# Layer 0 of a graph network: TensorE fetches part of the rows that GpSimd gathers

## The reference

```python
h = x @ W
e = leaky_relu((h @ att_src)[src] + (h @ att_dst)[dst], 0.2)   # edges and self loops
e = exp(e - segment_max(e, dst)[dst])
alpha = e / segment_sum(e, dst)[dst]
x = layernorm(x + tanh(segment_sum(h[src] * alpha[:, None], dst) + bias))
h1 = gelu(x @ W_pre + b_pre)
y = x + segment_sum(h1[src] * edge_attr, dst)
x = layernorm(x + y + gelu(gelu(y @ W1 + b1) @ W2 + b2))
```

## Time and profile before

| | us |
|---|---|
| median of 3 runs (3724.31 to 3727.02) | 3726.49 |
| the profiled execution | 3724.54 |
| its span, first to last instruction | 3722.8 |
| GpSimd busy in the span | 2781.1 (75%) |
| VectorE busy | 2438.3 (65%) |
| TensorE busy | 2393.6 (64%) |
| ScalarE busy | 1283.2 (34%) |

### The profile page before, as it was taken

One profiled execution on the slowest core, in us unless ns is written; L12 is line 12 of the kernel. 1 busy time (PEld: TensorE's weight loads), 2 busy tenths in 40 slices (PEclk: granted clock), 3 DMA queues, 4 the chain that ended last, 5 costly groups with the idle time before them and its releaser, 6 DMA issues.

```text
span 3722.8 us, 66966 instructions
## 1 busy us (share of the span) xinstructions
PE 2393.6 (64%) x16704; PEld 1951.7 (52%) x16705; DVE 2438.3 (65%) x6240; ACT 1283.2 (34%) x3893; POOL 2781.1 (75%) x2950
## 2 busy tenths in 40 slices
PE   6433343434344444444445988989888989999888
PEld 3333333333333333333334777777776777777776
DVE  7444444444466666566666777777777788888886
ACT  5433343434445555555553111111111221111222
POOL 7777777777777777777775777777777777777776
PEclk7555555555555555555557999999999999999998
DMA  5222221222222222222223343443334343444332
GB/s 102 43 42 42 41 44 42 44 42 43 42 43 44 43 44 43 43 44 45 44 45 99 93 94 90 95 94 94 95 91 96 93 96 91 97 95 99 93 95 70
DMA packets 351632, 254.26 MB, mean 68 GB/s; under 512 B 254125, under 2 KB 279218, under 8 KB 351387
## 3 DMA queue, kind: packets, MB, share of 16 engines
q0 software_dynamic: 94016, 146.16, 17.8%
q1 hardware_dynamic: 242753, 99.71, 11.7%
q10 hardware_dynamic: 14618, 6.14, 0.6%
HBM read 244.43 MB, written 7.25 MB: 68 GB/s over the span
## 4 chain that ended last, share of the span: by engine, by line
POOL 60%; issue 24%; ACT 4%; DVE 4%; PE 3%; DMA 2%; ACTq 1%; DVEq 1%; POOLq 0%; SPq 0%
POOL rows L690 60%; ACT onehot L747 1%; DMA rows<-table,src_i 1%; DMA src_i<-in_src_dram 1%; PE bank L1086 1%; ACT L790 1%; ACTq L740 0%; ACT pair L767 0%; DVE score L1361 0%; PE bank L1029 0%; PE bank L962 0%; ACT rowu L796 0%; DVE bst L1399 0%; ACT unused L790 0%; DVE newp L1352 0%
## 5 line engine op out<-in xcount | busy, mean ns | idle before, releaser
L690 POOL DMA_INDIRECT rows<-table,src_i x2850 | 2694.8, 946 | 896.0 <-issue 859.5
L1086 PE MATMUL bank<-node,hot 128*128 128x288 bf16 x9310 | 1228.4, 294 | 28.1 <-issue 16.5
L995 PE MATMUL bank<-onehot,rows 128*97 128x72 f32 (+1 forms) x3048 | 584.9, 369 | 814.9 <-ACT onehot L777 814.9
L1086 PEld LDWEIGHTS bank<-node,hot 128*128 128x128 bf16 x9310 | 932.2, 101 | 282.4 <-issue 20.9
L995 PEld LDWEIGHTS bank<-onehot,rows 128*97 128x97 f32 x3048 | 530.8, 281 | 854.4 <-issue 792.5
L1505 DVE TENSOR_SCALAR hot<-node,key 128x642 bf16<-128x642 int16 x1862 | 870.3, 539 | 130.8 <-PE bank L1086 80.0
L900 ACT ACTIVATE pair<-dst_i 128x8 f32<-128x8 int32 x196 | 35.2, 180 | 1175.3 <-DVE rows L1531 904.3
L747 ACT ACTIVATE onehot<-iota,far_dst 128x72 f32 (+1 forms) x1564 | 384.4, 328 | 23.0
L1339 DVE SCALAR_TENSOR_TENSOR other<-onehot,bank 128x576 f32<-128x576 f32 (+1 forms) x196 | 121.9, 622 | 404.1 <-ACT bank L760 335.4
L1073 PE MATMUL bank<-onehot,rows 128*96 128x40 f32 (+1 forms) x3128 | 306.8, 256 | 88.4 <-DVE rows L1536 50.6
L1073 PEld LDWEIGHTS bank<-onehot,rows 128*96 128x96 f32 x3128 | 295.8, 170 | 110.1 <-issue 88.7
(11 more groups left out here) (204 smaller groups left out, 1931.1 us busy)
## 6 DMA issues: line engine op xcount, KB each, us to landing
attr<-in_edge_attr_dram SPq DMA_DIRECT2D x190, 336.0 KB
rows<-table,src_i POOLq DMA_INDIRECT x2850
node<-in_src_dram SPq DMA_DIRECT2D x195, 64.0 KB
attr<-in_edge_attr_dram SPq DMA_DIRECT2D x190, 48.0 KB
dst_i<-in_dst_dram SPq DMA_DIRECT2D x200, 4.0 KB
src_i<-in_src_dram SPq DMA_DIRECT2D x195, 4.0 KB
src_i<-in_src_dram SPq DMA_DIRECT2D x190, 3.5 KB
dst_i<-in_dst_dram SPq DMA_DIRECT2D x190, 3.5 KB
```

What stands on the lines that cost most here:

```text
L690: pool.indirect_dma_start(rows[:, u, j * width:(j + 1) * width], None, table, bass.IndirectOffsetOnAxis(ap=src_i[:, u, j:j + 1], axis=0))\
L995: last = pe.matmul(total[:, 0:w], rows0(u, it)[:, j, 0:D1], wide(weights, w)[:, j, :], start=j == 0, stop=j == most - 1)
L1086: last = pe.matmul(p_got[t], hot[:, c % HOTS, i, t * P:(t + 1) * P], tab[:, a, :, :].rearrange("p k d -> p (k d)"), start=a == 0, stop=a = ...
```

## The change

Layer 0 gets what layer 1 has. From round 4 on, TensorE fetches the last tile of the first two groups in a narrow round and of the first group in a wide one (`BOOKED0 = 2`, `booked_in`), and GpSimd gathers seven tiles of those groups (`booked0`).

- In rounds 1 and 2 `table0` is split into three bf16 parts in nine steps, one a group (`split0` on ScalarE, `split_rest0` on VectorE); the parts lie in `attr`, behind `x1` and in `hot`.
- Each round's fetch is made one round ahead, in ten pieces of 4 or 5 blocks (`PIECE0`), two a group. VectorE compares for one piece between L1344 and L1318 of the next group, and for the other at that group's end (`marks0`); TensorE multiplies both behind the group's last half sum (`fetch0`; 3 x 98 columns). At the end of a round VectorE waits for the last piece and adds the three parts into tile 7 of the slot (`taken0`); ScalarE's `given` of a booked group waits for that.
- SyncE loads the 128 (256) source indices of the fetched tiles, the same row to all partitions (`load_src0`), and ScalarE shortens them to 16 bits (`shorten_src0`). The indices of a booked group come in three loads instead of two (`load_split`).
- Two PSUM banks are made free: `p_topb` and `p_newp` move into bank 0, `p_node2` into bank 6, and TensorE's chunk work waits for ScalarE's Gelu of the chunk before.
- Rounds 0 to 3 are written out instead of 0 and 1, and the last two instead of the last; chunks are held until round 4 (`HELD`).

```diff
+BOOKED0 = 2
+FROM0 = 4
+ERA0 = 10
...
-        p_top, p_topb, p_newp = bank[0][0:WIN, 0:P], bank[1][:, 0:WIN], bank[1][:, P:P + WIN]
+        p_top, p_topb, p_newp = bank[0][0:WIN, 0:P], bank[0][:, P:P + WIN], bank[0][:, P + WIN:P + 2 * WIN]
...
-        p_node, p_node2 = bank[6], bank[7]
+        p_node, p_node2 = bank[6], bank[6]
+        p_got0 = [bank[i][:, 0:3 * D2] for i in (1, 7)]
...
+        def booked_in(e, w):
+            return BOOKED0 if narrow(e, w) else 1
+        def booked0(it, u, w):
+            return in_era(it) and u < booked_in(it, w)
+        def fetched_at(it, u, w):
+            return booked_in(era_at(it, u), w)
+        def era_at(it, u):
+            return it + 2 if u == SLOTS - 1 else it + 1
+        def pieces_at(u):
+            return (0, 1) if u == SLOTS - 1 else (2 * u + 2, 2 * u + 3)
...
-                    for j in range(TILES - (e is e1 and booked(it, u))):
+                    for j in range(TILES - (booked(it, u) if e is e1 else booked0(it, u, ws[0]))):
...
+                if booked0(it, u, w):
+                    act.wait_ge(q_out, it - FROM0 + 1)
                 act.activation(p_src, rows0(u, it)[:, :, D1], ACT.Copy).then_inc(t0.given, 1)
...
+            def split0(k):
+                if k > 0:
+                    act.wait_ge(h_rest, k)
+                    act.activation(table0_part(k - 1)[:, :, 1, :], table0_left(k - 1), ACT.Copy).then_inc(h_mid, 1)
+                if k < len(TABLE0):
+                    if TABLE0[k][2] is flat[2]:
+                        act.wait_ge(e0.free, 2 * SLOTS + SLOTS)
+                    act.activation(table0_part(k)[:, :, 0, :], table0_rows(k), ACT.Copy).then_inc(h_hi, 1)
+            def shorten_src0(it):
+                act.wait_ge(q_src, 16 * BOOKED0 * (it + 3 - FROM0))
+                if not first_era(it, SLOTS - 1):
+                    act.wait_ge(q_hot, (it + 2 - FROM0) * ERA0)
+                act.activation(src16_0, src_all0, ACT.Copy).then_inc(q_src16, 1)
...
+            def fetch0(it, u, c, n):
+                pe.wait_ge(q_hot, piece_no(it, u, c) + 1)
+                if c == 0:
+                    if first_era(it, u):
+                        pe.wait_ge(h_tab, len(TABLE0))
+                    else:
+                        pe.wait_ge(q_out, it + 2 - FROM0)
+                for i, a in enumerate(range(PIECE0[c], PIECE0[c + 1])):
+                    for t in range(n):
+                        last = pe.matmul(p_got0[t], hot0[:, c % HOTS, i, t * P:(t + 1) * P], table0_block(a),
+                                         start=a == 0, stop=a == NB - 1)
...
                 window_sum(p_acc0, onehot[:, u, :], it, u, range(TILES // 2, TILES), w).then_inc(e0.acc, 1)
+                if in_era(era_at(it, u)):
+                    for c in pieces_at(u):
+                        fetch0(it, u, c, fetched_at(it, u, w))
...
+            def taken0(it, n):
+                v.wait_ge(q_done, (it + 2 - FROM0) * ERA0)
+                for k in range(n):
+                    last = v.tensor_reduce(rows0(k, it + 1)[:, TILES - 1, :], p_got0[k].rearrange("p (k d) -> p d k", k=3),
+                                           AX.X, ALU.add)
+                last.then_inc(q_out, 1)
+            def marks0(it, u, c, n):
+                if c == 0:
+                    v.wait_ge(q_src16, it + 3)
+                if not first_era(it, u) or c >= HOTS:
+                    v.wait_ge(q_done, piece_no(it, u, c) - HOTS + 1)
+                for i, a in enumerate(range(PIECE0[c], PIECE0[c + 1])):
+                    last = v.tensor_scalar(hot0[:, c % HOTS, i, 0:n], src16_0[:, 0:n], key[:, a:a + 1], None,
+                                           ALU.is_equal)
+                last.then_inc(q_hot, 1)
...
+                if ahead:
+                    marks0(back, at_u, pieces_at(at_u)[0], fetched_at(back, at_u, w) * P)
                 top_node(st, t0, g + 1, w)
...
+                    if split_step(it, u) is not None:
+                        split_rest0(split_step(it, u))
+                    if ahead:
+                        marks0(back, at_u, pieces_at(at_u)[1], fetched_at(back, at_u, w) * P)
+                    if u == SLOTS - 1 and in_era(it + 1):
+                        taken0(it, booked_in(it + 1, w))
```

More of the change, by code:

```diff
@@ L693, in gather @@
                 return body
-            groups(pool, gather(e0, table0, D2), alone=2)
+            groups(pool, gather(e0, table0, D2), alone=FROM0, apart=1)
             pool.wait_ge(m_st, STORED)
@@ L861, in middle_due @@
                 table_for(ACT.Exp, 3)
-            groups(act, weights, middle_due, alone=2)
+            groups(act, weights, middle_due, alone=FROM0, apart=1)
             rest(act, middle, middle_last)
@@ L1037, in _ @@
             spread_top(t0, 1, SLIM)
-            groups(pe, attend, alone=2)
+            groups(pe, attend, alone=FROM0, apart=1)
             def unread(n):
@@ L1495, in _ @@
             v.sem_inc(f_var, 1)
-            v.tensor_copy(key[:, :], key_i[:, :])
             def marks(it, c):
```

171 lines of the change are left out of this document (142 added, 29 removed).

## The result

The changed kernel takes 3732.58 us (median of 20 runs, 3730.24 to 3739.70), the kernel before 3725.26 (20 runs beside them): ratio 1.0021, 95% interval 1.0014 to 1.0028. Forecast were 3749.5 and "slower"; it is slower, by 7 us instead of 24. The profiled execution of after, 3739.7, is the slowest of its 20 and 15.2 above that of before (3724.5). Of these 15.2, 4.7 lie in layer 1 (1760.0 us from layer 0's last group to the end, 1755.3 before), which the change doesn't touch and which took 1755 to 1760 in the other kernels' profiled executions too. The median run is 7 us shorter than the profiled one; in which stage, no trace shows.

The account below looks back on a forecast made before the run. The prediction took GpSimd's gathers to bound layer 0, at 1.25 us each, while the arithmetic keeps up. Profiled 3724.5, plus 50 (wide rounds), minus 25 (narrow rounds), gave 3749.5 us, own range 3720 to 3785, chance 0.48.

Parts of the forecast that it names:

- Narrow part: Layer 0's 15 narrow rounds: 37.5 us of gathers saved, some 12 us of delay handed on, so -25 us.
- the terms costed at nothing: Layer 0: table split in rounds 1 and 2, new code, SyncE's loads, index shortening, held chunks, Gelu wait, shared banks: 0.
- a narrow group that catches up: Narrow rounds: 7.9 us a group, between VectorE's 7.25 and TensorE's 9.5 at half clock.
- Rival 2: Narrow rounds: TensorE stays at half clock, 54.7 us a round, 3872 us in all; chance 0.08.
- Wide part: Layer 0's 20 wide rounds: arithmetic grows from 925 to 1,050 us and replaces the gathers' 1,000 as the limit, +50 us.
- the price of the comparisons: VectorE's comparisons for the fetch: 0.19 us each at 128 columns (bounds 0.16 and 0.46), 0.25 at 256.
- the second place: Comparisons at the end of VectorE's group, with nothing waiting there: 5 x 0.19 + 0.1 = 1.05 us a wide group.
- The lower bound, from top_diag: One comparison of 128 columns on VectorE: 0.16 us apart in a row, from top_diag's shortest, 0.234 us long.
- The last group without a chunk: End of a wide round: second-place comparisons, wait for TensorE's last piece and reduction, +1.05 + 1.45 + 0.45 - 0.2 = +2.75 us.
- rival 1: Wide rounds: comparisons are short, only 4.3 us more a round, so the kernel gets faster, 3697 us; chance 0.32.
- Rival 3: Layer 0: all added work fits under the gathers, the full 62.5 us are saved, 3662 us; chance 0.05.
- Rival 4: Layer 0: 1,715 comparisons hold GpSimd up, its gathers lose 189 us, 3851 us in all; chance 0.07.

Follow-up runs that it names:

- narrow_only: The changed kernel with fetching ended at round 19, so wide rounds fetch none: narrow rounds took 719.5 us in all, the wide ones 1000.2.
- late_slots: The changed kernel with fetched tiles in a round's last groups and their reduction behind the next round's first group: wide rounds took 1002.6 us instead of 1035.5.
- late_few_marks_3: late_slots with 10 comparisons a round instead of 49 from the fifth round's pieces on (fetched tiles wrong): wide rounds took 980.0 us.
- few_marks: The changed kernel with one comparison kept per piece, 10 instead of 49 a round (fetched tiles wrong): wide rounds took 1005.3 us instead of 1035.5.

## Why the prediction was right in sign and wrong in size

*Narrow part, forecast -25.* Round 19 starts 25.6 earlier, but that is luck: two errors cancel. The narrow stage itself gained 30.7, and rounds 0 to 3 lost 5.1, which the prediction put at nothing. There GpSimd's first indirect gather starts 1.8 us later (108.1 against 106.3) and its 89th 4.5 later (220.9 against 216.4); which of the terms costed at nothing does that, no run separates. And a narrow group that catches up was priced at 7.9 us, where the middle groups of rounds 10 and 14 took 6.6 to 7.3. Rounds 5 to 8, ahead of the first chunk, took 47.4 to 48.4 (47.5 forecast) with the clock at 0.73 (0.6 to 0.9 forecast), those with a chunk 57. Rival 2 is out.

*Wide part, forecast +50.* Measured +36.1, shown by narrow_only to be all of it. The mechanism held: the arithmetic takes over, GpSimd waits for slots. Rounds take 47.0 without a chunk (47.3 forecast) and 55.0 with one (56.5). 8 x 47.0 + 12 x 55.0 = 1,036 against the forecast 1,050 of arithmetic.

*The step that failed: the price of the comparisons*, taken as 0.19 us for one of 128 columns and 0.25 for 256, and as 5 x 0.19 + 0.1 = 1.05 at the second place. The change's 1,715 comparisons start 0.163 and 0.196 apart (medians), and the 0.1 for a wait isn't there: five take 0.81 from their start to the next group's (1437.88 to 1438.69), 0.80 in the mean of 4.9. A middle group got 0.5 to 0.7 us longer instead of 0.85. The first four groups together took 1.3 to 1.4 us a round less than forecast, some 26 us over 19 rounds. The lower bound, from top_diag, would have been right, and its median misled: a row's shortest instance, in a row of its like, is the price of one in a run.

*A term left out, of the other sign.* The last group without a chunk got +3.8 instead of +2.75. Of its parts 1.50 (1.45 forecast) and 0.46 (0.45) were right, the comparisons 0.8 (1.05). Missing were 1.3 us of idle time. The prediction named the due table's load and the jump as queued behind the wait, but gave them no price: 0.66 for the load and branch, which no longer run beside VectorE's work, and 0.66 for the longer jump. ScalarE's part, put at nothing, was nothing here by the rows above. In rounds with a chunk the last group got +2.9, nearly as forecast.

So the sign was partly luck. With 0.80 at the second place, the prediction's own working gives a wide round 3 x 0.6 + 0.9 + 2.5 = 5.2 more, just under the 5.3 at which rival 1 takes over, and the sum is 3724.5 + 24 - 25 = 3723.5: neither slower nor faster. The comparisons that were priced too high stood in for the term that was left out.

*What the experiments add.* late_slots shows the reduction's place to be worth 33 us; with 39 comparisons fewer besides (late_few_marks_3) 55.5 are gone, down to about GpSimd's bound. What the comparisons alone are worth isn't shown, since few_marks has its own stop.

*Rival 1* needed a wide round under +5.3; it got (1035.5 - 925) / 19 = 5.8. *Rival 3* (everything fits) is what late_few_marks_3 comes near to, without most comparisons. The prediction's remark that 0.09 us a comparison would keep the wide arithmetic under 975 doesn't follow from its working: 3 x 0.35 + 0.55 + 2.25 = 3.85 us a round bring 925 to 998. *Rival 4* is 90 ns on the 46 gathers beside five comparisons of 256 columns, and less on others. The remaining 4.7 us of the profiled execution are layer 1's.

## What to carry over

When a wait is put into an engine's queue, price what stands behind it in that queue too: table loads and branches that ran beside the engine's work before are now in the open. A reduction that could have stood one group later cost 33 us over 19 rounds. A releaser named by a timeline is a candidate: compare its end with the start that it is said to release. An edit that leaves instructions out can bring a stop of its own, so look for idle time without a releaser before reading the run's time. And where a buffer holds one round, compare the arithmetic with the gathers round by round: here the fetch paid in the narrow rounds, where the slack was, and not in the wide ones.

## What the hardware showed

The distance of one-source VectorE instructions in a row splits into a fixed part and the columns (medians): 0.163 at 128 and 0.196 at 256 columns (26 ns per 100 columns), 0.201 at 156 and 0.256 at 260 in the one-port form (53 per 100), 0.454 at 642 in layer 1. All leave 0.12 to 0.13 us at no columns. The Trainium skill, "VectorE: DVE Perf Modes", section on the TRN2 errata, gives 58 cycles (0.06 us) for that part in its table and says below it that a single instruction shows about 150 (0.16 us); what these rows show lies between the two. Its columns per cycle agree.

From VectorE's branch at a loop's end to its sequencer's next record pass 2.7 us in the kernel before and 3.4 in the change (wide rounds without a chunk), with nothing in the profile that it waits for. Rounds 36 and 37 of the change, written out, have neither the jump nor idle time at their end.
